# Half of a round's gathers wait for one VectorE step more, in both attentions' score loops

## The reference

```python
# GAT scores (own edge list, 288 groups of 128 edges)
e = leaky_relu(a_src[src] + a_dst[dst], 0.2)        # 16 numbers for each edge
e_max = segment_max(e, dst)
# HGT scores (416 groups of 128 edges, 4 heads of 64)
attn_score = sum(q_att[etype, col_idx] * k[row_idx], axis=-1)
m = segment_max(score, col_idx)
alpha = exp(score - m[col_idx]) / denom[col_idx]
agg = segment_sum(alpha[..., None] * msg_edge, col_idx)
```

## Time and profile before

| | us |
|---|---|
| runs, median (lowest to highest of 3) | 5765.59 (5760.42 to 5766.13) |
| span of the one profiled execution | 6191.8 |
| GAT scores in it, 1291 to 1790 us | 499 |
| HGT scores in it, 2392 to 3130 us | 738 |
| HGT sums over edges in it, 3277 to 3503 us | 226 |
| counts in it, 541 to 900 us | 359 |

### The profile page before, as it was taken

One profiled execution on the slowest core, in us unless ns is written; L12 is line 12 of the kernel. 1 busy time (PEld: TensorE's weight loads), 2 busy tenths in 40 slices (PEclk: granted clock), 3 DMA queues, 4 the chain that ended last, 5 costly groups with the idle time before them and its releaser, 6 DMA issues. The chain is left out here.

```text
span 6191.8 us, 76002 instructions
## 1 busy us (share of the span) xinstructions
PE 4533.9 (73%) x22806; PEld 3190.3 (52%) x22842; DVE 3374.5 (55%) x7236; ACT 1645.9 (27%) x3766; POOL 2414.1 (39%) x2719
## 2 busy tenths in 40 slices
PE   5877978757758694566558889998999495354468
PEld 1223434545546452444436677777888363344456
DVE  8988972645556654677757743342111333544454
ACT  0964652411213251011100133333222121100022
POOL 0851018545540534555500028861122301577710
PEclk8988989868878897666758989999999697677779
DMA  0002447422232388777746410004333332233310
GB/s 31 2 11 102 190 181 210 157 45 39 41 60 79 100 322 277 236 246 240 242 132 218 149 25 12 17 7 129 100 110 120 91 100 61 91 91 90 92 29 21
DMA packets 413215, 696.03 MB, mean 112 GB/s; under 512 B 116843, under 2 KB 301299, under 8 KB 408203
## 3 DMA queue, kind: packets, MB, share of 16 engines
q1 hardware_dynamic: 316322, 440.23, 22.7%
q0 software_dynamic: 96320, 250.79, 13.5%
q10 hardware_dynamic: 192, 0.15, 0.0%
HBM read 450.69 MB, written 239.64 MB: 111 GB/s over the span
## 5 line engine op out<-in xcount | busy, mean ns | idle before, releaser
L1109 PE MATMUL wsum_a_ps<-wsum_a_hot,wsum_a_rows 128*128 128x128 f32 x1664 | 290.4, 349 | 359.7 <-DVE big L1136 185.7
L2242 POOL DMA_INDIRECT big<-hgt_table,edge_key x416 | 394.2, 948 | 364.4 <-DVE hgt_s_tmp L2335 221.0
L1095 POOL DMA_INDIRECT wsum_a_rows<-table,edge_src x416 | 434.2, 1044 | 221.9 <-issue 165.5
L1109 PEld LDWEIGHTS wsum_a_ps<-wsum_a_hot,wsum_a_rows 128*128 128x128 f32 x1664 | 272.1, 257 | 378.0 <-issue 210.0
L3928 PE MATMUL sagel_ps<-sagel_piece,sagel_high 128*128 128x448 f32 x1050 | 399.0, 380 | 0.8 <-issue 0.8
L3928 PE MATMUL sagel_ps<-sagel_piece,sagel_low 128*128 128x448 f32 x1050 | 385.2, 367 | 0.0
L2325 DVE TENSOR_REDUCE hgt_highest<-hgt_s_pm 128x8 f32<-128x1024 f32 x208 | 253.3, 1219 | 188.3 <-remote 181.6
L2242 POOL DMA_INDIRECT big<-gat_table,own_src x288 | 272.5, 946 | 211.6 <-issue 82.0
L2292 PE MATMUL hgt_s_pq<-big 128*128 x1248 | 249.9, 372 | 136.0 <-DVE hgt_s_tmp L2335 75.6
L2282 PE MATMUL hgt_s_pm<-hgt_s_turned,pick 112*128 112x128 bf16 x1664 | 188.5, 282 | 216.9 <-DVE hgt_highest L2325 185.3
L790 PE MATMUL cnt_ps<-cnt_hot_s,cnt_hot_d 128*128 128x512 bf16 (+1 forms) x1724 | 309.8, 333 | 39.0 <-DVE cnt_hot_s L772 34.9
(11 more groups left out here) (1007 smaller groups left out, 10909.7 us busy)
## 6 DMA issues: line engine op xcount, KB each, us to landing
hgt_edge_values<-big SPq DMA_DIRECT2D x104, 512.0 KB
big<-hgt_edge_values SPq DMA_DIRECT2D x104, 512.0 KB, 4.6
x<-counts SPq DMA_DIRECT2D x75, 448.0 KB, 3.3
x<-counts SPq DMA_DIRECT2D x75, 336.0 KB, 2.9
counts<-big SPq DMA_DIRECT2D x25, 832.0 KB, 3.4
counts<-big SPq DMA_DIRECT2D x25, 768.0 KB, 3.3
big<-counts SPq DMA_DIRECT2D x30, 640.0 KB
counts_turned<-big SPq DMA_DIRECT2D x30, 640.0 KB
```

The costliest lines, as they stand in the source:

```text
L1095: nc.gpsimd.indirect_dma_start(rows[n % DEEP][:, u, :], None, table, bass.IndirectOffsetOnAxis(ap=e.src[:, g:g + 1], axis=0)).then_inc(gat ...
L1109: mm = nc.tensor.matmul(ps[r.slot % 2][u][:, k * P:(k + 1) * P], rows[r.slot][:, u, k * P:(k + 1) * P], hot[r.slot % 2][:, u, :], start=Tr ...
L2242: nc.gpsimd.indirect_dma_start(rows[n % DEEP][:, u, :], None, at.table, bass.IndirectOffsetOnAxis(ap=at.index[:, g:g + 1], axis=0)).then_i ...
```

## The change

A round's third gather (u == R // 2) now waits also for `third` of round n - 4, VectorE's last step of the round that used the same ring place before; the fourth stands behind it on POOL. Beside that, each value that a semaphore is compared with and that comes from a register goes through a bitwise and first, which leaves it as it is and costs one register instruction each: 440 on VectorE, 416 on TensorE and 75 on ScalarE.

```diff
@@ -98,6 +98,11 @@
+def not_below_zero(value, highest):
+
+    return value & ((1 << highest.bit_length()) - 1)
@@ -768,7 +773,7 @@  (build_counts, VectorE)
-                            dve.wait_ge(moved, buckets[u] + 1)
+                            dve.wait_ge(moved, not_below_zero(buckets[u], 2 * NT - 1) + 1)
@@ -802,7 +807,7 @@  (build_counts, ScalarE; the same in edge_sums)
-                    wait_alone(act, done, end + BASE)
+                    wait_alone(act, done, not_below_zero(end, visits) + BASE)
@@ -2239,6 +2244,8 @@  (edge_scores, GpSimd)
                     for u in range(R):
                         g = n * R + u
+                        if n >= DEEP and u == R // 2:
+                            pool.wait_ge(third, n - DEEP + 1)
                         nc.gpsimd.indirect_dma_start(rows[n % DEEP][:, u, :], None, at.table,
@@ -2981,7 +2988,7 @@  (edge_sums, TensorE)
-                            pe.wait_ge(moved, blocks[u] + 1)
+                            pe.wait_ge(moved, not_below_zero(blocks[u], NT - 1) + 1)
```

More of the change, by code:

```diff
@@ L2994, in _ @@
                     end, = numbers(nc, mybir.EngineType.Activation, e.end[0:1, t:t + 1], groups)
-                    wait_alone(act, done, end + BASE)
+                    wait_alone(act, done, not_below_zero(end, groups) + BASE)
                     nc.scalar.copy(acc[:, t, :], part).then_inc(copied, 1)
```

## The result

The changed kernel takes 5773.51 us (median of 20 runs, 5767.63 to 5783.99), the kernel before 5764.77 on the same chip (20 runs, 5755.89 to 5776.72). The ratio is 1.0016, 95% interval 1.0010 to 1.0022: slower by 0.16%, inside what the prediction called no change, and 2.5 us above the time that it gave.

What follows compares the result with a forecast made beforehand. No engine was held full in the score stages; VectorE pauses on TensorE's late completions, mostly attributed to recording. Terms 0 + 5.7 + 0 + 0 = +5.7 us gave 5771 us, range 5690 to 5800.

Steps and rivals of the forecast that it cites:

- most of these pauses are not in the timed runs: HGT and GAT scores, weighted sum: VectorE's pauses without a named cause, 556 us over the run, come mostly from recording.
- 514 us of pauses for 426 us of gap: Removable pauses in HGT, GAT and the weighted sum, at most 514 us, nearly all needed to explain the longer profiled execution.
- the counts' window grew: Sign against the prediction: the counts' window, expected to stay at 359 us, gets longer.
- the third gather 0.27 us behind line 2375: Expected sign in HGT's timeline: the third gather starts 0.27 us after line 2375 ends, GpSimd's waits naming that line.
- Shorter pauses in the profile and yet no faster: Sharpest sign: HGT's profiled window may shrink by some 56 us while the timed runs do not move.
- The wait binds: HGT's third gather goes later because of the added wait: 1.41 us in a quick round, 5.2 with a pause.
- The cover of 12.7 us: Slack left for the delayed gathers' transfer before VectorE's product reads them; cost zero, or 73 us if the cover went.
- The DMA engines' 5.39 us as the least round: HGT scores: without pauses a round goes down to the DMA engines' own work, 5.39 us, a gain of 177 us.
- HGT sums +5.7: TensorE's ands in the HGT sums: 0.11 us each, half paid per round, 5.7 us in all; ends 1.7 and 11.4.
- Counts 0: VectorE's 440 ands in the counts: hidden under 629 ns instructions, so zero; 48 us without that cover.
- The first rival: Pauses are real and the wait shortens each by 1.16 us: HGT 56 us, GAT 18, giving 5697 us; chance 0.28.
- the second rival: Pauses in HGT and GAT are real and go altogether: up to 177 + 133 us, giving 5461; chance 0.05.

Runs made afterwards that it cites:

- experiment 1: Changed kernel without the third gather's added wait, bitwise ands kept, on chip 9 against the kernel before: 6121.57 us against 6115.09, ratio 1.0018.
- experiment 2: The changed kernel as it is, on chip 0, a chip with pauses, against the kernel before: 6151.03 us against 6187.03, ratio 0.9943.
- experiments 6 to 8: Chip 11 against the kernel before: changed kernel again, 1.0019; without the added wait, 1.0017; with the wait at a round's first gather, 1.0020 and 1.0016.
- experiment 5: Changed kernel without the added wait, three ands per HGT sums product on TensorE instead of one, chip 0: 6268.36 us, ratio 1.0128 against the kernel before.
- experiment 10: Changed kernel with HGT's wait at a round's first gather, GAT's replaced by a memset after each gather; chip 4: 6081.30 us, ratio 0.9949 against before.

## Why the prediction was right, and where not

**The time was right, its main reason was not.** The prediction decided on "most of these pauses are not in the timed runs" since recording makes them. Its conclusion holds for the runs measured, its reason fell with experiment 1: span and timed run are equal on both kinds of chip (5768.2 and 5770.04; 6118.6 and 6120.45). By all that is on record the 426 us were the difference between two chips. That the result was taken on a chip without pauses was luck: on chip 0 the same change is 36 us faster, and the forecast of no change would have missed. The sum that seemed to support it, 514 us of pauses for 426 us of gap, showed at most that the pauses are in one measurement and not in the other. Its terms were not sound either: HGT gained 190 us and not 177 at most, and the weighted sum 66 and not 203.4, since a wait that goes is partly replaced by another. It could not say which of the two things that differed, the profiler or the chip, was the cause; I named only the first. The profiled executions, as long as the runs beside them, fit what the Trainium skill's "NOTIFIC — the notification-queue block", section 6.1, says: that a record costs no more than its own write. Section 7.1 of the same page of the Trainium skill says that the block holds its producers back rather than lose a record inside; whether that has a part in the pauses on chips 9, 0 and 4, no run here shows, and the trace of 5768.2 us has no pauses.

**The prediction's own signs.** It called itself wrong if the counts' window grew, and it did, from 332.3 to 335.8 us. Its other mark, the third gather 0.27 us behind line 2375, did not come in the result's trace, only on chip 0. "Shorter pauses in the profile and yet no faster" came true for another reason than the one given: trace and runs of the change are both without pauses.

**"The wait binds"**: right where there are pauses (3.76 us of idle time ended by it in experiment 2), wrong where the result was taken. It was read off a trace in which GpSimd is ahead after each pause; without pauses its own 1.25 us a gather keep it behind. The wrong step cost nothing here, as its price was put at zero either way. (That GpSimd runs "1.35 us later" follows from no row; 2704.11 - 2702.70 is 1.41.)

**The cover of 12.7 us**: consistent with experiments 6 to 8, in which the wait, even at the first gather, costs nothing; its length was not measured.

**The DMA engines' 5.39 us as the least round**: too high. It was 0.76 of a window with pauses, 561 us of work; without them it is 0.98 of 548 us, 537, and in the stage's middle the round is 5.08 us. So share times length moved by 4% at the same number of bytes and is an estimate, not a floor.

**HGT sums +5.7**: +6.2 measured. The term was sized by a third of a 0.33 us stretch, paid by half. That the size came out does not show the working: experiment 5 has 0.09 us for each further instruction, of all four products and without the half, so the near hit is partly luck.

**Counts 0**: this term was mis-sized: 3.5 us measured (3.3 to 5.3 over all traces with one and), and 28.6 for twice as many more. The 2.4 us of idle time before the long instruction were read as cover. Cover there is in a row of long instructions, but it ends where another engine waits for the first of them: TensorE's waits for it are 34.9 us in 41 places before, 37.0 in 45 after, 59.2 in 66 with three ands. I looked at what the instruction waits for and not at who waits for it. How much of the 28.6 us goes this way is not separated; the waits grew by 22.2.

**The first rival** had its mechanism right on a chip with pauses: 8.28 us until VectorE stops, 8.23 worked out. Its size was twice too large in HGT (-29 against -56): it took the number of pauses as fixed, and shorter ones came more often, 52 for 40. In GAT -16 against -18 is luck: the "remote" waits at the maximum, which the rival counted, did not shrink (75.8 and 81.3 us without the wait, 98.3 with it); those of the experts' line 2499, now 2506, did, from 53.0 and 47.9 to 12.3. Of the second rival, that the pauses go altogether, only experiment 10's GAT stage shows anything, and there it took a break behind every gather.

**Open**: why TensorE's completions come late during gathers on some chips and not on others. That it is the chip, and not the hour or what else ran beside it, is itself only likely: each of chips 9, 0 and 4 served once, chip 11 twice with the same time. The granted clock is lower where the pauses are (HGT 0.69 against 0.81, GAT 0.83 against 0.92) and not elsewhere (counts 0.97 and 0.98, sums 0.99 and 0.98); which of the two brings the other was not tried. And before was not profiled on a chip without pauses; for +6.2 and +3.5 us that matters little, as the stages with one and are equal on all chips.

## What to carry to other kernels

Before explaining why a span differs from timed runs, ask whether both come from the same chip, and look for a stage that the change can't touch: if it moved as well, the kernel's change is not the reason. A wait whose end has no known cause is not yet lost time: compare the lengths of the stage. A wait on a queue is worth only what it ends last by, so read where its engine stands when it gets there, in the state that will be measured. One register instruction may hide under a long one; count what the sequencer does for each long instruction before a second is added.

## What the runs showed of the hardware

- The same program takes 5760 to 5765 us in the result's runs and on chip 11, and 6112 to 6187 on three other chips. Between one trace of each kind 382 of 424 us are in the three stages with dense gathers (GAT, HGT, the weighted sum), in which VectorE waits for completions of TensorE.
- An indirect gather of 128 rows is issued each 1.25 us, with 20 numbers in a row (GAT) as with 512 (HGT), and on chips 9 and 0 pauses come with both. On chip 4, where GAT's gathers stood 1.5 us apart, GAT had none.
- A register instruction on TensorE's sequencer ahead of a product of 382 ns costs 0.015 us as the first extra one and 0.09 each as the second and third; on VectorE's, ahead of 629 ns, 0.008 to 0.012 and 0.033 us.
